# Twelve of sixteen layer-0 steps in three rounded passes, four scaled chunks a tile, and block-diagonal fields written by ScalarE

## The reference

```python
for W, b in params:                                   # (128, 64*64), (128, 128*64), (128, 128*64)
    z = jnp.einsum('bhd,bfd->bhfd', x_vec, input)     # outer product with the input, per sample and element
    B, h, f, d = z.shape
    z = z.reshape(B, h * f, d)
    x_vec = jnp.einsum('oc,bcd->bod', W, z) + b[None, :, None]
    outs.append(x_vec.sum(axis=2))
return jnp.concatenate(outs, axis=1)                  # (512, 3 * 128)
```

## Time and profile before

| | |
|---|---|
| median of 3 runs | 1118.36 us (1117.12 to 1119.52) |
| profiled execution, its own time | 1118.71 us |
| its span (first to last instruction) | 1117.0 us |
| busy: PE, DVE, ACT, POOL | 1071.4, 857.4, 717.8, 867.2 us |
| mean granted TensorE clock | 0.995 of full |

### The profile page before, as it was taken

How to read it: one execution, slowest core, us unless ns; L and a number is a source line. 1 busy time by engine, 2 the same in 40 slices (tenths; PEclk the granted TensorE clock), 3 DMA queues, 4 the chain that set the end, 5 groups by cost and what they waited for, 6 DMA issues and landing times.

```text
span 1117.0 us, 17733 instructions
## 1 busy us (share of the span) xinstructions
PE 1071.4 (96%) x4781; PEld 804.3 (72%) x4781; DVE 857.4 (77%) x2518; ACT 717.8 (64%) x2433; POOL 867.2 (78%) x727
## 2 busy tenths in 40 slices
PE   4879999999999999999999999999999999999997
PEld 3767677777768777777778777777777877777676
DVE  5565788878794787888885788888887588887982
ACT  4456676767673676767674576766766477676781
POOL 3456898988985789897977679797988579799560
PEclk9999999999999999999999999999999999999998
DMA  6752423223231231423332133333222232321000
GB/s 253 200 120 76 93 76 73 77 55 95 64 86 53 51 98 52 97 71 81 88 67 58 45 85 83 67 94 75 77 57 74 57 74 77 73 76 46 1 22 8
DMA packets 108325, 85.87 MB, mean 77 GB/s; under 512 B 71040, under 2 KB 73824, under 8 KB 108096
## 3 DMA queue, kind: packets, MB, share of 16 engines
q1 hardware_dynamic: 105680, 73.98, 27.4%
q10 hardware_dynamic: 2544, 10.75, 2.8%
HBM read 14.75 MB, written 0.79 MB: 14 GB/s over the span
## 4 chain that ended last, share of the span: by engine, by line
PE 84%; DVE 7%; ACT 5%; issue 2%; DMA 1%; POOL 1%; ACTq 0%; DVEq 0%
PE y L875 57%; PE l L895 10%; PE l L875 7%; PE xt L986 5%; DVE acc L762 3%; PE l2p L998 3%; ACT prod L650 2%; ACT y L639 1%; DVE bd L718 1%; DMA gram<-in_L_rec_W_dram 1%; DVE acc L747 1%; DVE x1l L728 1%; DVE gram L835 1%; PE l2p L975 1%; ACT x1h L548 0%
## 5 line engine op out<-in xcount | busy, mean ns | idle before, releaser
L762 DVE SCALAR_TENSOR_TENSOR acc<-y,x0t,acc 128x128 f32<-128x128 f32 x1792 | 493.2, 340 | 69.3 <-PE y L875 63.2
L650 ACT ACTIVATE prod<-y,x0t 128x128 f32<-128x128 f32 x1280 | 368.9, 381 | 232.7 <-PE y L875 225.8
L875 PE MATMUL y<-w1h,x1h 128*128 128x512 f32 x1024 | 466.5, 456 | 13.9 <-DVE acc L762 11.8
L875 PE MATMUL y<-w1h,x1l 128*128 128x512 f32 x1024 | 402.4, 393 | 0.0
L875 PE MATMUL y<-w1l,x1h 128*128 128x512 f32 x1024 | 401.2, 392 | 0.0
L441 POOL TENSOR_TENSOR z<-z,xg 128x512 f32<-128x512 f32 (+2 forms) x272 | 372.6, 1374 | 14.2 <-DMA z<-xg 13.9
L451 POOL TENSOR_TENSOR pacc<-pacc,prod 128x512 f32<-128x512 f32 x192 | 253.0, 1318 | 138.5 <-ACT prod L650 138.5
L875 PEld LDWEIGHTS y<-w1h,x1h 128*128 128x128 f32 x1024 | 193.4, 189 | 115.9 <-issue 45.7
L639 ACT ACTIVATE y<-y,x0t 128x128 f32<-128x128 f32 x768 | 215.9, 350 | 74.0 <-PE y L875 73.9
L747 DVE TENSOR_TENSOR acc<-y,acc 128x512 f32<-128x512 f32 x192 | 132.6, 691 | 136.7 <-ACT y L639 133.1
L875 PEld LDWEIGHTS y<-w1l,x1h 128*128 128x128 f32 x1024 | 193.1, 189 | 59.1 <-issue 29.1
(11 more groups left out here) (93 smaller groups left out, 664.2 us busy)
## 6 DMA issues: line engine op xcount, KB each, us to landing
z<-xg SPq DMA_DIRECT2D x480, 128.0 KB, 2.4
w2t<-in_L_rec_W_dram ACTq DMA_DIRECT2D x8, 512.0 KB, 12.3
gram<-in_L_rec_W_dram ACTq DMA_DIRECT2D x8, 512.0 KB, 4.4
xg<-in_r_input_dram SPq DMA_DIRECT2D x30, 128.0 KB, 3.9
z<-xg SPq DMA_DIRECT2D x32, 96.0 KB, 2.5
z<-xg SPq DMA_DIRECT2D x15, 192.0 KB
gram<-in_L_rec_W_dram ACTq DMA_DIRECT2D x1, 2048.0 KB, 10.3
out_dram<-z SPq DMA_DIRECT2D x4, 192.0 KB, 1.9
```

Source lines behind the costliest of these rows:

```text
L650: last = nc.scalar.activation(prod[:, h % HSLOTS, k, :], y[c % YB][:, k * O:(k + 1) * O], ACT.Copy, scale=x0t[:, j, f:f + 1])
L762: ins = nc.vector.scalar_tensor_tensor(out=to, in0=of, scalar=x0t[:, j, f:f + 1], in1=b1r[:] if m == 0 else to, op0=ALU.mult, op1=ALU.add)
L875: ins = nc.tensor.matmul(to, stationary, moving, start=(first and k == 0), stop=(last and k == 2))
```

## The change

- PARTED becomes 1, 2, 3, 5, 6, 7, 9, 10, 11, 13, 14, 15: twelve steps in three passes, four whole (0, 4, 8, 12). The zh is made seven positions ahead of PE's step and the zl five (for the products of group 1: five and three; in group 0: both one).
- Room for the longer weight tables: z has five slots instead of six (group 0: LSLOTS 6 instead of 8), zl keeps two, zh has three and takes in zleft as the thirteenth use in turn. DVE's zl therefore now waits for its own slot.
- SCALED becomes (3, 6, 9, 15): chunk 6 goes from four DVE multiply-adds to four ACT multiplications and one DVE addition. SCALED_LAST stays.
- `own_rows` moves from DVE (one instruction of 128 x 256) to ACT (four of 128 x 64), at the same position, now in front of ACT's own chunk work.
- PRODUCTS_AT: POOL makes one more product in the second tile and none in the fourth.

```diff
-ZSLOTS = 6
+ZSLOTS = 5
-PARTED = tuple(range(1, 15, 2))
+PARTED = tuple(t for t in range(ZT - 1) if t % 4)
-ZHSLOTS = 2
+ROUNDED = PARTED + (ZT - 1,)
+RN = len(ROUNDED)
+ZHSLOTS = 3
+ZLSLOTS = 2
-SCALED = (3, 9, 15)
+SCALED = (3, 6, 9, 15)
-LSLOTS = 8
+LSLOTS = 6
-LATER_PARTED_AT = [{t: LATER_AT[t] - k for t in PARTED} for k in (2, 1)]
-PARTED_FIRST_AT = [{AHEAD_FIRST_AT[t] - k: t for t in PARTED} for k in (6, 4)]
-PARTED_AT = [{AHEAD_AT[t] - k: t for t in PARTED} for k in (6, 4)]
+LATER_PARTED_AT = [{t: LATER_AT[t] - k for t in PARTED} for k in (1, 1)]
+PARTED_FIRST_AT = [{AHEAD_FIRST_AT[t] - k: t for t in PARTED} for k in (5, 3)]
+PARTED_AT = [{AHEAD_AT[t] - k: t for t in PARTED} for k in (7, 5)]
-PRODUCTS_AT = ((2, 1, 1, 1, 1), (1, 1, 1, 1, 1), (1, 1, 1, 1, 1), (1, 0, 0, 0, 0))
+PRODUCTS_AT = ((2, 1, 1, 1, 1), (2, 1, 1, 1, 1), (1, 1, 1, 1, 1), (0, 0, 0, 0, 0))
...
-                    if t == 2:
+                    if t == (ZSLOTS * GROUP - (ZT - 1) * P) // (GROUP - P):
                         sp.wait_ge(prep_made, W0_STEPS)
...
+            def slot_of_parts(n, t):
+                i = rounded(n, t)
+                if i >= ZHSLOTS:
+                    before = i - ZHSLOTS
+                    act.wait_ge(z_used, ZT * (before // RN) + ROUNDED[before % RN] + 1)
+                return i % ZHSLOTS
...
+                    if c == OWN_AT:
+                        own_rows(tile, j)
                     if c in HELPED:
                         multiply(tile, j, c)
...
+            def own_rows(tile, j):
+                act.wait_ge(l2p_made, layer2_ready(tile - 2))
+                act.wait_ge(own_made, 1)
+                for b in range(HALF_B):
+                    last = nc.scalar.activation(bd[:, j % 2, b * F:(b + 1) * F], x0t[:, j, :], ACT.Copy,
+                                                scale=own_half[:, b:b + 1])
+                last.then_inc(bd_made, 1)
...
+                if i >= ZLSLOTS:
+                    before = i - ZLSLOTS
+                    dve.wait_ge(z_used, ZT * (before // PN) + PARTED[before % PN] + 1)
                 dve.wait_ge(zh_made, i + 1)
...
-                nc.vector.tensor_tensor(bd[:, j % 2, 0:GRAM].rearrange("p (b f) -> p b f", f=F),
-                                        x0t[:, j, :].unsqueeze(1).to_broadcast(shape),
-                                        own_half[:].unsqueeze(2).to_broadcast(shape), ALU.mult).then_inc(bd_made, 1)
```

More of the change, by code:

```diff
@@ L261, in weights @@
                 tiles = [t for t in PARTED if t // 4 == r]
-                i, step = PARTED.index(tiles[0]), tiles[-1] - tiles[0] if len(tiles) > 1 else 1
+                i, step = PARTED.index(tiles[0]), tiles[1] - tiles[0] if len(tiles) > 1 else 1
                 return to[:, i:i + len(tiles), :], y[w0_bank(r)][:].rearrange("p (t o) -> p t o", o=O)[
@@ L265, in weights, with rounded, zhslot, zleft @@
             return w0left[rows, :], y[w0_bank(r)][rows, 0:O]
+        def rounded(n, t):
+            return RN * n + ROUNDED.index(t)
+        def zhslot(n, t):
+            return rounded(n, t) % ZHSLOTS
+        def zleft(n):
+            return zh[:, zhslot(n, ZT - 1), :]
         def z_rows(t):
@@ L505, in _ @@
                 act.dma_start(w1raw[:, part], w1[:, part]).then_inc(w1_loaded if k < W1_FIRST else w1_rest_loaded, 16)
+            def slot_of_parts(n, t):
[4 more added lines that the diff above has]
+                return i % ZHSLOTS
             def part_upper(n, t):
-                i = PN * n + PARTED.index(t)
                 cols = LATER if n == 0 else slice(0, GROUP)
                 act.wait_ge(z_made, ZT * n + t + 1)
[L512 to L515, removed]
+                slot = slot_of_parts(n, t)
+                nc.scalar.copy(zh[:, slot, cols], zin(n, t)).then_inc(zh_made, 1)
             def left_parts(n):
@@ L522, in left_parts @@
                 act.wait_ge(z_made, ZT * n + t + 1)
-                if n > 0:
-                    act.wait_ge(z_used, ZT * n)
-                nc.scalar.copy(zleft[rows, cols], zin(n, t)[rows, :]).then_inc(left_made, 1)
+                slot = slot_of_parts(n, t)
+                nc.scalar.copy(zh[rows, slot, cols], zin(n, t)[rows, :]).then_inc(left_made, 1)
             def fields(n, tiles, first):
@@ L662, in _ @@
                     rows = slice(0, z_rows(ZT - 1))
-                    nc.scalar.copy(zleft[rows, EARLY], l2p[rows, i % 2, EARLY]).then_inc(early_left_made, 1)
+                    nc.scalar.copy(zleft(0)[rows, EARLY], l2p[rows, i % 2, EARLY]).then_inc(early_left_made, 1)
             act.wait_ge(w0sum_made, 3)
@@ L707, in left_lower @@
                 cols = LATER if n == 0 else slice(0, GROUP)
[L708 removed]
+                part = zleft(n)[LOWER_UPPER, cols]
                 nc.vector.tensor_tensor(part, zin(n, ZT - 1)[LOWER_UPPER, :], part.bitcast(F32),
                                         ALU.subtract).then_inc(left_lowered, 1)
[L712 to L720 removed]
             def lower(n, tiles):
@@ L883, in layer0 @@
                     pe.wait_ge(left_lowered, n + 1)
-                    nc.tensor.matmul(l0[:, cols], w0left[0:rows, :], zleft[0:rows, cols], start=False,
+                    nc.tensor.matmul(l0[:, cols], w0left[0:rows, :], zleft(n)[0:rows, cols], start=False,
                                      stop=True).then_inc(z_used, 1)
@@ L949, in early_layer0 @@
                 pe.wait_ge(early_left_lowered, 1)
-                nc.tensor.matmul(l0[:, EARLY], w0left[0:rows, :], zleft[0:rows, EARLY], start=False,
+                nc.tensor.matmul(l0[:, EARLY], w0left[0:rows, :], zleft(0)[0:rows, EARLY], start=False,
                                  stop=True).then_inc(early_l0_made, 1)
```

21 lines of the change are left out of this document (6 added, 15 removed).

## The result

The changed kernel takes 1125.33 us (median of four runs, 1124.83 to 1127.83) against 1117.74 us (1116.31 to 1119.52) for the kernel before in the same runs: a ratio of 1.0071, with a 95% interval of 1.0058 to 1.0083. It is slower by 7.6 us. The forecast was 1096.5 us, with a range of 1090 to 1107.

What follows compares the result with a forecast made beforehand. PE, busy 96% of the span, was taken to bound the kernel, with a once-a-group wait for DVE second. 1118.7 - 17.2 - 0.6 + 1.1 - 7.5 + 2 = 1096.5 us; range 1090 to 1107.

Steps and rivals of the forecast that it cites:

- term 6: Group 0's first two tiles: 2 us net cost beyond the 0.6 won, bounds -2 and +5.
- Term 1: PE's layer-0 steps: five going from whole to three passes save 0.23 us each, 17.2 us over groups 1 to 15.
- rival D: PE's parted steps: the first of three passes costs more, so 0.05 of each 0.23 us goes, 4 us, inside the range.
- Term 2: PE's wait for DVE at the group's end: about 0.5 us less per group, 7.5 us, bounds 0 to 13.
- Term 3: ACT's new load: 9.8 us per inner group, bd 0.8 per tile, ACT 52.8 busy, covered by banks, cost nothing.
- Rivals A and B: A: ACT late, gain at group's end lost, 1104, chance 0.24; B: ACT bounds the dense stretch, 1111, chance 0.10.
- Term 4: DVE's load: five zl added, four bd and part of chunk 6 removed, net -0.1 us per group, unchanged.
- rival C: POOL and DVE hold each other, delaying ACT's casts and PE by 2.1 us per group; 1126 us, chance 0.04.
- Term 5: z slots and POOL's stream: z ready ahead of ACT's need, by 0.6 to 1.5 us, covered narrowly; cost nothing.
- the forecast's sign: Group 0, sign for term 6: the first y of position 16 near 71 to 73 us.
- The last line of the list of signs: Mid-group: the forecast would be wrong if PE waited at a layer-0 step for zl; no size given.

Runs made afterwards that it cites:

- b_bd_act: The kernel before with only bd (own_rows) moved from DVE to ACT; 1114.96 us, 0.9975 of the kernel before.
- a_bd_dve: The changed kernel with bd (own_rows) back on DVE at its old place and in its old form; 1133.37 us, 1.0138 of the kernel before.
- a_pool16: The changed kernel with POOL's z products, additions and two of three combining instructions cut to 16 columns; 1107.26 us, 0.9908 of the kernel before.
- a_zl16: The changed kernel with each zl from group 2 on cut to 16 columns, POOL working in full; 1105.22 us, 0.9881 of the kernel before.
- a_zl4: The changed kernel with every zl one position later, four instead of five ahead of PE's step; 1130.17 us, 1.0108 of the kernel before.
- a_zl15_pool: The changed kernel with step 15's zl made by POOL after its last z product (groups 2 to 15); 1109.52 us, 0.9922 of the kernel before.
- a_parted7: The changed kernel with only the parted steps put back to the seven odd ones; 1117.92 us, 1.0003 of the kernel before.

## Why the prediction was wrong

Between the spans the forecast was 28.8 us too low (22.2 promised, 6.6 lost). The eleven short groups make 22.0 of it (2.00 each on average), the three long ones 3 x 1.07 = 3.2, group 0 3.4 (of which more under term 6), and the stretch after the last group's start 0.3.

**Term 1, five steps on PE: right.** The parted step with its chunk takes 0.20 to 0.22 us less per step, once 0.17, where the sum had 0.23; that is 1.0 instead of 1.15 per group. The chain shows the pieces as in the earlier trace rows, 0.68 or 0.69 for the step and 2.04 to 2.06 behind it. What is missing is 2 us in all, half of rival D's 4; whether it is D was not looked at.

**Term 2, the wait at the group's end: right.** 0.41 instead of 0.5 per group. bd was all of it: b_bd_act and a_bd_dve move the end by 0.75 and 0.74. Chunk 6 was worth nothing; it only moves what is left of the wait from position 4 to position 0.

**Term 3, ACT: right in its sum (52.9 busy in a group, forecast 52.8), slightly low in bd.** In ACT's timeline four bd take 1.19 us from the first's start to the next instruction:

```profile
583.59 1.19 ACT L658 ACTIVATE bd<-x0t,own_half 128x64 f32<-128x64 f32 x4
584.78 1.14 ACT L679 ACTIVATE prod<-y,x0t 128x128 f32<-128x128 f32 x4
```

The estimate was 0.8, its upper bound 1.1. By the Trainium skill's price ("ScalarE: Activation LUTs", What ACT_TABLE_LOAD costs) the estimate was 1.0, which is nearer: in the trace one bd starts 0.24 us after the other, as by that price, but the next instruction only about 0.5 after the last. bd on ACT does cost something that the sum had at nothing: 9-14 lengthens by 0.17 to 0.19 in every kernel that has it, save a_pool16, a_zl16 and a_zl4 (5.84). It is the wait at position 12 behind the zl of step 1, so it is holding too, and no lack of ACT's time. Rivals A and B, both by ACT, did not happen: DVE ends PE's waits.

**Term 4, DVE: this is the step that failed.** Two assumptions in it were wrong.

The first is the length of a zl: "five zl (0.83 mean each)". The mean was taken over to a kernel in which DVE and POOL meet in another way. It measured 1.13 for all twelve, so DVE got 4.1 us more work per group instead of none. The spread of the earlier trace rows was the sign that 0.83 is no property of the instruction but of the meeting: 679 to 1172 ns for the 512-column form. (The 545 that rival C quotes for equal work is of the 384-column form, and so is the 0.99 of z, which for 512 columns takes at least 1.26.)

The second is heavier: the new zl were counted as load and never placed. The text looked at what DVE waits for ahead of them, and of what stands behind them it said: "Behind it are queued only the next chunks." Those next chunks were the point. Step 15 is made at position 52; five positions ahead is 47. Chunk 47 (c = 15) is scaled, so DVE gets to it only after ACT (571.51 to 572.71, idle 1.10), then makes the zl, and then chunk 48, whose bank PE wants for chunk 52. DVE could begin chunk 48 at 573.3 and needs 1.1 us for it; PE, whose last pass began at 574.47, could start chunk 52 at 574.7. That is 0.3 us of slack for an instruction of 0.6 from start to start. With an unheld zl the stretch is 0.5 us too long (a_pool16), with a held one 1.3. By the order of the code none of the other eleven stands between a scaled chunk and four multiply-adds at the very next position, and with step 15 whole the group is 1.1 us shorter. Two more of them, unheld harmless, leave PE no slack once held for about a microsecond: those of steps 5 and 1, 0.3 and 0.2 us per group.

**Term 5, z and POOL: right as far as it went.** ACT waited 11.1 us in all, 31 times, for z (34.8 before, 29 times). POOL's products were in time, though POOL, held in its turn, was busy 1.7 us longer per group.

**Term 6, group 0: over its upper bound in this execution, and only in part by the change.** By the sum the first inner group would have started 0.85 us later (0.6 won, 1.1 and 2 lost, and group 0's share of terms 1 and 2, 1.65), at most 3.85; it started 4.24 later. The first tile's float32 products took 6.91 us instead of 5.16. In a_zl15_pool, whose group 0 has the same instructions, they took 6.27, that is 0.11 for each of the ten added, as the sum had it:

```profile
26.89 6.91 PE l L964 x56
```
```profile
26.89 6.27 PE l L988 x56
```

In the changed kernel's execution the first seven of the 56 start 0.21 us apart, the others 0.11. After that its granted clock was at the lower of its two levels (1.2 instead of 2.4 GHz) for 3.4 us at 38.4 and again at 75.9. The window (us, busy of PE, PEld, DVE, ACT, POOL, granted clock):

```profile
75.90:79.30 3.40, 3.40 (x13) 2.73 (x12) 1.31 (x5) 0.23 (x1) 3.32 (x4) 0.50 0.81 203
```

PE had stood still for 1.95 us just ahead of 75.58; in the kernel before it stood as long at this place (1.96, up to 73.50) and the clock did not fall. The kernel before has one such stretch in group 0, at 35.5, and a_zl15_pool none. There the first inner group starts at 137.22: 2.7 us earlier than in the changed kernel, and 1.5 later than before. Against the kernel before, the changed one is 2.1 us later at position 16 (75.6, where the forecast's sign was 71 to 73), 3.5 at position 18, behind the slow stretch, and 4.2 at the end; in the last part, among others, a zl of 1.75 us stands (114.35). What the change costs in group 0 at an equal clock was not measured.

**Rival C** had the right mechanism, and got a chance of 0.04. Its path was wrong, so that its time (1126; measured 1125.3) is right by luck. It sent the delay through POOL's stream to ACT's casts, late by 2.1 us per group. In fact POOL's stream lost little (a z product takes 1392 ns on average, 1374 before) and DVE's instruction was held in a place without slack. The argument used against it, that only one such instruction more stands in a group (eleven to twelve), is refuted twice: by a_parted7, where seven zl are as long as twelve, and by the total of held time, which went from 36 to 86 us.

The last line of the list of signs was the right one to look for, but in the wrong place: PE did come to wait in the middle of a group, not at a layer-0 step for zl (3.8 us in the whole run) but at a chunk for a bank that zl kept from being freed.

**What stays open.** The mean of zl jumps when bd leaves DVE (817 to 935 in the kernel before, 1002 to 1127 in the changed one) and again from b_bd_act to a_parted7. The traces show the nearer cause: a zl ends 0.55 us after the POOL instruction under way (last section), and on average that one still had 0.26 us to go in the kernel before, 0.38 in b_bd_act, 0.46 in a_bd_dve, 0.58 in a_parted7 and 0.60 in the changed kernel. Why DVE comes to its zl at other moments of POOL's stream was not isolated. The waits at 23 and 12 are still in a_zl15_pool (4.63 and 6.01); moving the zl of steps 5 and 1 was not tried.

## What to carry to other kernels

An instruction that is added to an engine with spare time has to be placed, not only counted: list what stands right behind it, which buffer that frees, and when the bounding engine wants it back; one zl of twelve, at one place, cost 12.8 us while the engine was idle a tenth of the time. If the same instruction shows a wide spread of durations for equal work, price it at the long end wherever it stands on such a path, and ask which other engine it meets. Here the delay went away when the work was given to the engine that caused it (POOL made the zl itself), while moving every zl by a position passed it on.

## What the runs showed of the hardware

A DVE subtraction with both operands in SBUF is held by a busy POOL for a time that hardly depends on its own size. 16 columns took 0.16 us alone and 585 ns on average, 512 columns 0.68 alone and 1127 on average: 0.42 and 0.45 us held. It is held up to POOL's end: of the 168 zl of the changed kernel's inner groups 156 began while a POOL instruction had over 0.15 us to go, and all of these ended 0.54 to 0.56 us after it, however long it still ran. In the kernel before it is 73 of 98, all of them at 0.55 to 0.56. So a zl of 512 columns takes 0.68 us, or what POOL's instruction has left plus 0.55, whichever is more; this gives every one of the 168 and the 98 to within 0.03 us. DVE's instructions that read y (PSUM) and acc kept their length (L769, mean 690 ns; 691 before) with the same POOL beside them. It works the other way too: POOL's addition takes 1.29 us, and 1.75 when a zl was under way at its start (POOL's timeline, beside DVE's zl from 569.63 to 570.57):

```profile
569.97 1.75 POOL L465 TENSOR_TENSOR pacc<-pacc,prod 128x512 f32<-128x512 f32 x1
```

POOL made the same subtraction in 1.27 to 1.30 us, all 14 times (a_zl15_pool): work that takes DVE 0.68 alone is not much dearer there than the 1.13 that DVE needed beside POOL.
